# Layer 1 of a two-layer graph network: member matrices made by TensorE and ScalarE instead of VectorE

## The reference

```python
h = jnp.maximum(_layernorm(x, axis=-1), 0.0)
# layer 1, 4 heads of 32 channels
q = (h @ Wq + bq).reshape(n, H, C)
k = (h @ Wk + bk).reshape(n, H, C)
v = (h @ Wv + bv).reshape(n, H, C)
alpha = jnp.einsum('ehc,ehc->eh', q[dst], k[src]) / math.sqrt(C)
amax = jax.ops.segment_max(alpha, dst, num_segments=n)
ea = jnp.exp(alpha - amax[dst])
denom = jax.ops.segment_sum(ea, dst, num_segments=n)
alpha = ea / (denom[dst] + 1e-16)
out = jax.ops.segment_sum(v[src] * alpha[:, :, None], dst, num_segments=n)
x = x + out.reshape(n, H * C) + (h @ Wskip + bskip)
# layer 2: h again, then x + h_self + segment_sum((h[src] + edge part) * in_degree[dst], dst)
```

## Time and profile before

| | us |
|---|---|
| median of 3 runs | 1664.47 (1663.79 to 1665.09) |
| span of the profiled execution | 1662.8 |
| table stage, attention stage, message stage | about 300, 700, 650 |
| busy in the span: PE, DVE, ACT, POOL | 1470.4, 1347.6, 1016.5, 1083.1 |

### The profile page before, as it was taken

The page is one execution under the profiler, slowest core; times in us unless marked ns, Lnnn a source line. Parts: engine busy times, 40 slices in busy tenths (PEclk is TensorE's granted clock), DMA queues, the critical chain, the costliest instruction groups (busy, mean ns, idle before and its releaser), DMA issues. The chain is left out here.

```text
span 1662.8 us, 34477 instructions
## 1 busy us (share of the span) xinstructions
PE 1470.4 (88%) x10545; PEld 1263.5 (76%) x10546; DVE 1347.6 (81%) x3688; ACT 1016.5 (61%) x2501; POOL 1083.1 (65%) x1202
## 2 busy tenths in 40 slices
PE   5888898699999999999999974899998999998996
PEld 4666777688888888888888863777776777777775
DVE  8879665299999999999999994677776777777675
ACT  5777888556555565656665513566665666665663
POOL 2554442577777777777777605777777777777772
PEclk9999999899999999999999996999999999999999
DMA  8899887556666666666666516677666767667672
GB/s 219 274 274 313 284 300 262 157 160 180 189 174 192 175 188 183 178 182 182 182 174 185 156 45 148 148 160 174 162 163 150 171 160 172 161 158 170 149 164 68
DMA packets 162552, 302.85 MB, mean 182 GB/s; under 512 B 104113, under 2 KB 107703, under 8 KB 157524
## 3 DMA queue, kind: packets, MB, share of 16 engines
q1 hardware_dynamic: 121503, 201.19, 41.9%
q0 software_dynamic: 40896, 99.90, 24.9%
HBM read 196.84 MB, written 104.12 MB: 181 GB/s over the span
## 5 line engine op out<-in xcount | busy, mean ns | idle before, releaser
L803 POOL DMA_INDIRECT sb_kv<-kv_rows,sb_src_all x500 | 492.9, 986 | 187.1 <-issue 131.3
L831 POOL DMA_INDIRECT sb_kv<-x_rows,sb_src_all x500 | 473.8, 948 | 209.3 <-issue 109.1
L1710 ACT ACTIVATE sb_hn<-sb_xn 100x128 f32<-100x128 f32 x500 | 240.5, 481 | 265.9 <-DMA sb_kv<-x_rows,sb_src_all 225.1
L1713 ACT ACTIVATE sb_vw<-sb_kv 128x128 f32<-128x128 f32 x500 | 239.6, 479 | 0.0
L1638 ACT ACTIVATE sb_hn<-sb_xn,sb_nstat 100x128 f32<-100x128 f32 x500 | 231.5, 495 | 0.0
L1400 DVE COPY sb_hT<-ps_b 128x400 f32<-128x400 f32 x250 | 142.2, 569 | 96.1 <-PE ps_b L2005 95.3
L1797 PE MATMUL ps_b<-sb_w,sb_memberT 128*125 128x256 f32 x800 | 201.6, 391 | 18.3 <-DVE sb_xn L921 9.2
L1660 ACT COPY sb_memberT<-ps_b 100x512 f32<-100x512 f32 x150 | 75.8, 506 | 205.7 <-PE ps_b L1885 205.7
L1797 PEld LDWEIGHTS ps_b<-sb_w,sb_memberT 128*125 128x125 f32 x800 | 146.2, 193 | 41.7 <-issue 14.7
L2005 PE MATMUL ps_b<-sb_member,sb_vw 128*128 128x100 f32 x1000 | 173.8, 278 | 0.0
L2005 PEld LDWEIGHTS ps_b<-sb_member,sb_vw 128*128 128x128 f32 x1000 | 157.4, 198 | 9.8 <-issue 9.8
(11 more groups left out here) (184 smaller groups left out, 3103.0 us busy)
## 6 DMA issues: line engine op xcount, KB each, us to landing
kv_rows<-sb_kv SPq DMA_DIRECT2D x26, 1120.0 KB
sb_xn<-x_rows SPq DMA_DIRECT2D x50, 507.8 KB
sb_xn<-in_x SPq DMA_DIRECT2D x50, 500.0 KB
out_rows<-sb_xo SPq DMA_DIRECT2D x49, 500.0 KB
x_rows<-sb_xo SPq DMA_DIRECT2D x24, 1015.6 KB
sb_kv<-in_edge_attr SPq DMA_DIRECT2D x500, 32.0 KB
sb_kv<-in_x SPq DMA_DIRECT2D x28, 560.0 KB
kv_rows<-sb_xn SPq DMA_DIRECT2D x13, 1120.0 KB
```

Source lines behind the costliest of these rows:

```text
L803: pool.indirect_dma_start(out=kvs[:, k % 4, t, :], out_offset=None, in_=kv_rows, in_offset=bass.IndirectOffsetOnAxis(ap=src_all[:, n:n + 1 ...
L831: pool.indirect_dma_start(out=xs1[:, k % 4, t, :], out_offset=None, in_=x1, in_offset=bass.IndirectOffsetOnAxis(ap=src_all[:, n:n + 1], ax ...
L1710: nc.scalar.activation(hn1[:, t, :], xn1[:, k % 4, t, 0:D], ACT.Relu, scale=xn1[:, k % 4, t, D:D + 1], bias=xn1[:, k % 4, t, D + 1:XW]).th ...
L1713: nc.scalar.activation(hs1[:, t, :], xs1[:, k % 4, t, 0:D], ACT.Relu, scale=xs1[:, k % 4, t, D:D + 1], bias=xs1[:, k % 4, t, D + 1:XW]).th ...
```

## The change

The member matrix of a tile has a 1 where edge e goes to node n. It is now computed as Relu(1 - (d_e - n)^2): for whole numbers that is 1 where they are equal and 0 elsewhere. With both shifted by 50, 1 - (d - n)^2 = (1 - n^2) + 2dn - d^2, a product of a few factors that bf16 holds exactly when the two squares are split in parts. So each tile gets three rows on the edge side (d^2 in two parts, and d) and three on the node side (-1, -1 and 2n), and two rows shared by the batch carry 1 - n^2 in two parts; ten tiles fill 32 rows. Four batches lie beside each other on the 128 partitions.

- `members` of VectorE is gone (two instructions per batch, lines 1181).
- `turned_member` on TensorE makes the turned matrix directly, ten bf16 matmuls of 32 rows (100 columns of weights, 128 moving) in the place of ten fp32 transposes; ScalarE's copy of it becomes an ACTIVATE with Relu.
- `row_member` makes the plain matrix with two bf16 matmuls of 500 columns each, into banks 2 and 0, before and after `gather_q`'s first group; ScalarE writes it with two ACTIVATEs of 128x500 (`member_rows`) at the end of its step. `turn_h` now waits for the second of them, M1.
- Once, in the table stage: GpSimd fills the node parts (`node_parts`, five instructions), VectorE computes them and the edge parts (`const_row`, five; `drel_part`, six), SP moves them by DMA (1, 3, 3 and 24 DMAs, behind the table's loads and stores 23, 25, 27 and 29).
- A buffer of the path for long tiles (`masked`) moves into spare room; no tile of this input takes that path.

```diff
-N_ITEM = 8
-ITEM = {"h0": 1, "h1": 2, "q0": 3, "q1": 4, "m0": 5, "q2": 6, "m1": 7, "m2": 8}
+N_ITEM = 10
+ITEM = {"h0": 1, "h1": 2, "q0": 3, "q1": 4, "m0": 5, "q2": 6, "m1": 7, "m2": 8, "M0": 9, "M1": 10}
...
+            def edge_parts_in():
+                sp.wait_ge(drel_part_out, 16 * 3)
+                for quad in range(QUADS):
+                    cols = (BATCHES - quad + QUADS - 1) // QUADS
+                    for j in range(3):
+                        for first, last in ((0, cols - 1), (cols - 1, cols)):
...
+            def drel_part(n):
+                wait(dve, drel_part_step, n)
+                if n == 0:
+                    ins = dve.tensor_scalar(mid_drel, drel_f.rearrange("r g e -> r (g e)"), -1.0, NODES + 1.0,
+                                            ALU.max, ALU.min)
...
+                if m == 6 and n < 5:
+                    const_row(n)
...
+                if m == 12 and n < 6:
+                    drel_part(n)
...
-            def members(k, part):
-                first, last = ((0, 4), (4, B))[part]
...
-                dve.tensor_tensor(member[:, k % 3, first:last, :],
...
-                nc.scalar.copy(memberT[:, k % 2, first:last, :],
-                               banks[(1, 0, 1)[g]][0:NODES, 0:(last - first) * WIN]
-                               .rearrange("n (t e) -> n t e", e=WIN)).then_inc(A.evac, 1)
+                nc.scalar.activation(memberT[:, k % 2, first:last, :],
+                                     banks[(1, 0, 1)[g]][0:NODES, 0:(last - first) * WIN]
+                                     .rearrange("n (t e) -> n t e", e=WIN), ACT.Relu).then_inc(A.evac, 1)
+
+            def member_rows(k, i):
+                first, last = HALVES[i]
+                act.wait_ge(A.item, N_ITEM * k + ITEM[f"M{i}"])
+                wait(act, A.agg, 3 * (k - 2))
...
+                nc.scalar.activation(member[:, k % 3, first:last, :],
+                                     banks[(2, 0)[i]][:, 0:5 * NODES].rearrange("e (t n) -> e t n", n=NODES),
+                                     ACT.Relu).then_inc(A.evac, 1)
...
-                wait(pe, A.evac, N_ITEM * (k - 1) + ITEM[("m1", "m2")[i]])
+                wait(pe, A.evac, N_ITEM * (k - 1) + ITEM[("M1", "m2")[i]])
...
-                    ins = nc.tensor.transpose(banks[(1, 0, 1)[g]][0:NODES, (t - first) * WIN:(t - first + 1) * WIN],
-                                              member[:, k % 3, t, :], ident[:])
+                    ins = nc.tensor.matmul(banks[(1, 0, 1)[g]][0:NODES, (t - first) * WIN:(t - first + 1) * WIN],
+                                           of_node[:, t, :], of_edge, start=True, stop=True)
                 ins.then_inc(A.item, 1)
+
+            def row_member(k, i):
+                first, last = HALVES[i]
+                of_edge, of_node = parts(k)
+                pe.wait_ge(A.evac, N_ITEM * k + ITEM[("q2", "m1")[i]])
+                nc.tensor.matmul(banks[(2, 0)[i]][:, 0:5 * NODES].rearrange("e (t n) -> e t n", n=NODES),
+                                 of_edge, of_node[:, first:last, :], start=True, stop=True).then_inc(A.item, 1)
```

More of the change, by code:

```diff
@@ L397, in __init__ @@
                 self.evac = s("front_copied")
-                self.member = s("member_built")
                 self.qe = s("q_gathered")
@@ L1280, in step0 @@
             def step0(k):
-                this, prev, nxt = real(k), real(k - 1), real(k + 1)
+                this, prev = real(k), real(k - 1)
                 m = (k - 3) // 2
@@ L1304, in step0 @@
                 stats(4)
-                if nxt:
-                    members(k + 1, 0)
                 stats(5)
@@ L1331, in step0 @@
                 stats(13)
-                if nxt:
-                    members(k + 1, 1)
                 if prev:
```

137 lines of the change are left out of this document (122 added, 15 removed).

## The result

| | before | after |
|---|---|---|
| median, us | 1664.78 (1663.79 to 1665.88) | 1693.13 (1689.68 to 1694.08) |
| span of the profiled execution | 1662.8 | 1691.3 |
| first gather, end of the table stage | 300.46 | 313.98 |
| first to last multiplication of scores | 314.6 to 977.6 = 663.0 | 328.3 to 1006.8 = 678.5 |
| from there to the end of the span | 685.2 | 684.5 |

The changed kernel is slower: ratio 1.0154, 95% interval 1.0134 to 1.0175. The forecast was 1666 (1658 to 1681). The 28.5 us of span are 13.7 up to the first multiplication of scores (the table stage), 15.5 in the attention stage and -0.7 behind it, so two separate causes had to be found.

What follows compares the result with a forecast made beforehand. VectorE bounds the attention stage now; after the change a chain through three engines would, at 13.36 and 13.55 us a step. Span 1662.8 - 1 + 2.5 = 1664.3, median 1.7 above: 1666 us, range 1658 to 1681.

Steps and rivals of the forecast that it cites:

- What bounded before: Attention stage: VectorE full, members 1.17 us a step; without them other bounds lie close, the chain about 12.7.
- TensorE alone: Attention stage: TensorE's work stays about even (-0.05, upper end +0.44), about 12.1 us a step, no bound unless made to wait.
- x: Spacing of the bf16 matmuls that make turned tiles on TensorE: 0.06 us taken, upper end 0.109.
- Rival 1: Attention stage: VectorE the only bound, the chain doesn't close; step 12.6 us, 42 us less, 1622; chance 6%.
- The chain through three engines: Attention stage: waits through TensorE, ScalarE and VectorE close the step at 13.28 us, 13.47 with statistics, before dearer ACTIVATEs.
- M1 to `turn_h`: Chain term: from M1's start on ScalarE to `turn_h` on TensorE, 0.63 us, as `copy_h` to the projection.
- sum to weights: Chain term: softmax's sum to its weights on VectorE, 2.12 us, 2.31 in a statistics step.
- turn to the next tiles: Chain term on TensorE: weights' turn to next tiles 4 to 7, 5.34 us, from 5.65 with less idling for node sums.
- ACTIVATE for COPY: Four ScalarE instructions on the chain: 0.02 us dearer each, 0.08 a step, giving 13.36 and 13.55.
- The table stage: Before the attention stage: added fills, instructions and DMAs mostly hidden; bounds 0 and +6 us, +2.5 taken.
- 3 (a dear chain, 1681): Attention stage: tile spacing 0.109 and dearer ACTIVATEs add 0.31 us a step, about 1681, half-way 1673; chance 28%.
- 4 (the table pays, 1671): Table stage: loads or stores late behind the 24 DMAs, +6 us or more, chain as summed, 1671; chance 10%.

Runs made afterwards that it cites:

- e8: Kernel before, with VectorE's two member instructions left out from batch 3 on and nothing in their place (result not the reference's): ratio 0.9871 to the kernel before.
- e7: Changed kernel, `row_member` matmuls moved, third query group ahead of the first turned tiles, member matmuls over all 128 rows (wrong result): ratio 0.9931 to the kernel before.
- e3: Changed kernel with `turned_member` and `row_member` multiplying all 128 rows in place of 32 (wrong member matrices): ratio 1.0077 to the kernel before.
- e1: Kernel before's attention stage with all the change's added table-stage work, unused there: ratio 1.0075 to the kernel before.
- e14: Kernel before plus the added table-stage work, without the 24 inward and three outward edge-part DMAs: ratio 1.0014 to the kernel before.
- e10: Changed kernel with `row_member` and query group reordered, edge parts in fewer DMAs, node parts zero-padded to 128 rows: ratio 0.9873 to the kernel before, median 1648.34 us.
- e13: Kernel before plus the added table-stage work, without the 24 inward edge-part DMAs: ratio 1.0036 to the kernel before.

## Why the prediction was wrong, point by point

**What bounded before.** Right that the members' 1.17 us are not the gain; e8 gives 12.79 where the prediction had 12.7 for the chain without them. The agreement is partly luck: in e8's plain steps the weights are ready 0.18 us before TensorE takes them (608.23 and 608.41), so it was TensorE's sequence, put at 12.53 with its wait for `copy_h`, that gave the 12.79.

**TensorE alone: the term that failed.** It said that TensorE's work stays even (-0.05, at most +0.44) and is no bound. Without the wait for M1 its sequence is 13.46, and that of before is 12.79 (e8, where only `copy_h` holds it in a plain step): it rose by 0.67 us a step. The tiles were as cheap as taken (x = 0.06 predicted, 0.38 / 6 = 0.063), the wide matmuls as well (0.22 each). The rest is the passage from matmuls of 128 (or 100) rows to those of 32 and back: 0.09 ahead of the six tiles, 0.08 behind the first `row_member`, 0.22 ahead of the second and 0.09 behind it, 0.09 ahead of the four tiles and 0.10 behind them, 0.67 in all. That the step failed at this term and at no other of TensorE's, e7 shows: without passages, in the better order, the sequence is 12.76, 0.03 under that of e8, where -0.05 was predicted. The bound from above took the dearest distance between equal matmuls; a cost between unlike ones was not in it. The row of the bias matmul, bf16 among fp32 without a gap, made the type look harmless, rightly, but it has 128 rows like its neighbours and says nothing of a change in the row count. Rival 1 had 12.53 for the same sequence (12.1 and the wait for `copy_h`); 0.26 of its gap to 13.46 was in the starting point, the 12.79 of e8.

**The chain through three engines: right as far as `copy_h`, and not what closed the step.** The wait for M1 is there (0.24). Behind `copy_h` two paths lead to the weights' turn: the softmax through ScalarE and VectorE, which the prediction followed, and TensorE's own matmuls. An earlier plain step, the last VectorE instruction of the softmax and the turn:

```profile
444.08 0.28 DVE L1341 TENSOR_TENSOR sb_wr<-sb_er,sb_rtot 40x128 f32<-40x128 f32 x1
```

```profile
444.70 0.25 PE L2041 MATMUL ps_b<-sb_ident,sb_wr 40*128 40x40 f32 x1
```

The weights lay ready at 444.36, 0.34 us before TensorE took them, and the steps up to 505 us are 13.70 all the same. So the step is TensorE's sequence of 13.46 with its wait for M1, and the prediction's sum stands beside it:

| term | predicted | measured, 601.05 to 614.76 |
|---|---|---|
| tiles to m1 | 0.49 | 0.46 |
| m1 to M1 | 2.00 | 2.00 |
| M1 to `turn_h` | 0.63 | 0.73 |
| `turn_h` to `copy_h` | 0.62 | 0.65 |
| `copy_h` to exponential | 1.38 | 1.34 |
| exponential to sum | 0.36 | 0.33 |
| sum to weights | 2.12 | 2.35 |
| weights to their turn | 0.34 | 0.40 |
| turn to the next tiles | 5.34 | 5.45 |
| sum | 13.28 | 13.71 |

The measured terms follow one another from one step's tiles to the next one's, so they add up to the step whatever bounds it. M1's measured start is 603.04 plus its share of the pair, 0.47. M1 let `turn_h` go 0.14 after its end, where the projection starts 0.05 after a copy; that is the 0.10 in the third term, and it is unexplained. The 0.11 in the last term is the passage to 32 rows.

The 0.23 at the weights comes from one VectorE instruction (line 1336, 0.43 us long, where line 1230 took 0.22 before); in the stretch its mean is 388 ns against 263. GpSimd's gather was running beside it:

```profile
606.90 0.95 POOL L883 DMA_INDIRECT sb_kv<-kv_rows,sb_src_all  x1 [0.30 <-issue]
```

The gather ends at 607.85 and the VectorE instruction at 607.89. It is so each time: of the 45 between 340 and 960 us, the 33 that took over 0.3 us began 0.53 to 0.57 after a gather's start and all ended 0.04 to 0.05 behind that gather's end; the 12 that took less met no gather, or one that had begun at most 0.49 before them. Before, 12 of 46 were long, all in steps with statistics up to 655 us. Those steps are 13.85, the later ones, where it takes 0.22, are 13.71; so the 2.31 of the earlier trace rows holds this too, and the prediction's pair of 26.94 is one of the first half only (the mean step is 13.44). What makes one engine wait for the other no run here shows. In the changed kernel it costs little: it leaves the plain step at 13.70, where TensorE comes to the weights' turn no sooner (608.78 and four distances is 609.22, and such a turn starts 0.09 later in the earlier trace rows too), and makes TensorE wait 0.04 in steps with statistics, the 13.75 from 505 us on.

In e3 the prediction's chain does close the step: TensorE is relieved, waits 0.45 for M1 and in 34 of 46 steps for the weights, and the step is 13.32 where the instruction above takes 0.22, 13.42 where it takes 0.34 and 13.54 where it takes 0.46. So the sum of the prediction was right for a kernel without the passages.

**ACTIVATE for COPY.** Right, it costs next to nothing: 585 against 579 ns for 500 columns, 591 against 579 for 512, 372 against 360 for 256, 6 to 12 ns where 20 were taken. The hold of M0 was 0.47, as a copy's. The 186 ns + 0.833 ns a column of the Trainium skill ("ScalarE: Activation LUTs", "What ACT_TABLE_LOAD costs") would make an estimated 602 ns of the first, and a hold of 0.51: a little too much here. The 81 ns of the Trainium skill for a load and matmul of 128 columns ("TensorE: Matmul & The Clock Gate", "Back-to-back issue gap") is not what this trace shows, 63 ns with 32 rows and 55 with 128.

**The table stage: the second failed term.** Predicted +2.5 (0 to +6), measured +13.7. Three things were wrong in it. The cost of an issue, up to 0.43, was about right for the 24 (0.32 to 0.49 each but for one of 1.99, 11.6 with gaps), but the three outward ones, counted by their bytes, held the queue 10.1. "Mostly hidden" by a store slot's 20 us was argued and not read: what came late were the loads, and the gather by as much. And it was counted as if the parts hid one by one; e1 against e14 shows the 27 small DMAs outside the cover.

**The rivals.** The nearest was 3 (a dear chain, 1681) together with 4 (the table pays, 1671), but neither had its true size; the range ended where either of them held alone. Added up they would have given 1685 (1681 + 6 - 2.5), and for other reasons: neither the tiles nor the ACTIVATEs were dear.

**What the prediction wanted to see.** VectorE waiting for the exponential (0.47) and `member` ahead of `turn_h` (0.24) are there in plain steps, and plain and statistics steps are alike; but the first of the two waits did not lengthen the step; the first gather was later. Not foreseen was `row_member` as a brake of its own.

## What to carry to other kernels

When an engine at 94% busy gets new instructions, price the places between unlike ones, not only the run of like ones: here matmuls of 32 rows among matmuls of 100 and 128 cost 0.08 to 0.22 us at each edge, zeros in the unused rows took that away, and grouping them took away part. Many DMAs of small pieces cost more of a queue than their bytes say, and loads and stores behind them come late by what the queue's idle time doesn't cover. Where VectorE's small instructions and GpSimd's gathers run side by side, look at which ones end together. And taking work from the busiest engine is worth what the next two paths leave: leave the work out once, as in e8, before building its replacement.

## What was not expected of the hardware

- **Passage between row counts.** 0.08 to 0.22 us a time between matmuls of 32 and of 100 or 128 rows, with the idle time shown at the weight load; none with 128 rows throughout (e3, e7, e10), where 128 and 100 rows still alternate. Which 32 of the 128 partitions they are makes no difference: four batches take turns on them and the steps are 13.70 one after another. The Trainium skill ("TensorE: Matmul & The Clock Gate", "Why this matters for your kernels") says of a lone matmul "K=32 single mm = same time as K=128". Within a run of equal ones the trace nearly agrees (0.063 and 0.055 us); at the edges it does not.
- **Pieces of 256 bytes.** Three DMAs of 125 KB, 500 pieces each, held SyncE's queue for 10.1 us and put what followed 5 us back; one DMA with the same bytes in 500 pieces of 768 put it back by 1 us. The number of DMAs differs too.
- **24 DMAs of up to 120 pieces, 0.38 MB in all** held the queue for 11.6 us; of the whole they cost 6.5 us by the ratios of e1 and e13 and 2.4 by their medians. The Trainium skill ("DMA: Bandwidth & Descriptors", "Bandwidth") says "Transfers under 64 KB are descriptor-dominated"; the runs agree in kind.
- **A VectorE instruction that waits for a gather's end.** The TENSOR_SCALAR of 40x128 took 0.22 us, or ended 0.04 to 0.05 us behind the gather on GpSimd that had begun 0.53 to 0.74 us before it, up to 0.46 us in all; so it was in all 45 long cases of before and after. The scan before it (0.42) and the reciprocal behind it (0.94 to 0.95) kept their times.
